# Experts' up product: from full-precision matmuls to three single-pass products of split tiles, with the rows turned one block sooner

## The reference, cut to what matters

```python
E, K, D, I = 16, 2, 512, 384
# x: [1250, 512]; each node goes to its two best of 16 experts, and all to a shared one
h = rows @ expert_w1[e] + expert_b1[e]          # up product: [n, 512] @ [512, 768]
g = clip(h[..., ::2], -gate_clamp, gate_clamp)
u = clip(h[..., 1::2], -up_clamp, up_clamp)
t = g * sigmoid(g * alpha) * gate_scale * (u + up_shift)
y = t @ expert_w2[e] + expert_b2[e]             # down product: [n, 384] @ [384, 512]
out[node] += weight * y
```

## Time and profile before

| | |
|---|---|
| median of 3 runs | 908.85 us |
| the profiled execution | 910.05 us, span 908.3 us |
| mean granted clock of PE | 0.926 |
| PE busy | 811.4 us, 89% |
| DVE busy | 485.9 us, 53% |
| ACT busy | 250.2 us, 28% |
| POOL busy | 126.6 us, 14% |
| experts' up product, L1224 | 448 matmul records, mean 492 ns, 155.9 us |
| experts' down product, L1272 | 168 records, mean 605 ns, 78.6 us |
| chain that ended last | PE 70%, DVE 17%, DMA 6%; L1224 14%, L1272 7% |

### The profile page before, as it was taken

How to read it: one execution, slowest core, us unless ns; L and a number is a source line. 1 busy time by engine, 2 the same in 40 slices (tenths; PEclk the granted TensorE clock), 3 DMA queues, 4 the chain that set the end, 5 groups by cost and what they waited for, 6 DMA issues and landing times.

```text
span 908.3 us, 12470 instructions
## 1 busy us (share of the span) xinstructions
PE 811.4 (89%) x3696; PEld 583.8 (64%) x3697; DVE 485.9 (53%) x949; ACT 250.2 (28%) x502; POOL 126.6 (14%) x186
## 2 busy tenths in 40 slices
PE   4679699999999986948999958989999999999993
PEld 2555588888888863626888846887655555555551
DVE  6899481441341387899024685896343443434341
ACT  2455241331341103515221313421021222212121
POOL 2000000000000120000000500212123333333321
PEclk9985699999999995979999968979999999999997
DMA  2600000000000010000101102004698859663542
GB/s 112 205 1 2 1 1 1 0 1 1 1 1 1 29 40 9 1 1 1 47 1 53 58 1 92 22 1 176 218 355 248 297 136 367 167 180 57 135 92 32
DMA packets 32156, 71.34 MB, mean 79 GB/s; under 512 B 4254, under 2 KB 4504, under 8 KB 32110
## 3 DMA queue, kind: packets, MB, share of 16 engines
q1 hardware_dynamic: 25838, 56.04, 17.1%
q0 software_dynamic: 6272, 14.68, 8.1%
HBM read 96.53 MB, written 12.72 MB: 120 GB/s over the span
## 4 chain that ended last, share of the span: by engine, by line
PE 70%; DVE 17%; DMA 6%; issue 3%; ACT 2%; SPq 1%; ACTq 0%; DVEq 0%; POOL 0%; POOLq 0%
PE PS L994 20%; PE PS L1224 14%; PE PS L1024 9%; PE PS L1272 7%; PE PS L1117 5%; PE PS L1063 3%; DMA WB<-in_w 3%; PE PS L925 3%; DMA X<-in_x 3%; PE PS L1257 2%; DVE XN L1343 1%; PE PS L1208 1%; DVE ET L1396 1%; DVE ET L1391 1%; ACT CTR L693 1%
## 5 line engine op out<-in xcount | busy, mean ns | idle before, releaser
L994 PE MATMUL PS<-CTR,YH 125*128 125x500 f32 (+1 forms) x480 | 164.1, 357 | 2.3 <-DVE YL L1526 2.3
L994 PE MATMUL PS<-CTR,YL 125*128 125x500 f32 (+1 forms) x480 | 163.6, 356 | 0.0
L1224 PE MATMUL PS<-WB,YF 128*128 x448 | 155.9, 492 | 0.1
L1224 PEld LDWEIGHTS PS<-WB,YF 128*128 128x128 f32 x448 | 80.9, 190 | 65.7 <-issue 20.7
L994 PEld LDWEIGHTS PS<-CTR,YH 125*128 125x128 f32 x480 | 91.5, 191 | 15.5 <-DVE YL L1526 2.6
L994 PEld LDWEIGHTS PS<-CTR,YL 125*128 125x128 f32 x480 | 91.5, 191 | 13.1
L925 PE MATMUL PS<-ET 125*128 125x130 f16 x494 | 66.4, 302 | 21.1 <-DVE ET L1401 17.2
L1272 PE MATMUL PS<-WB,YF 128*128 x168 | 78.6, 605 | 1.6 <-DMA WB<-in_w 0.9
L925 PEld LDWEIGHTS PS<-ET 125*128 125x128 f16 x494 | 43.2, 128 | 45.0 <-DVE ET L1401 22.2
L1553 DVE TENSOR_TENSOR ZL<-PS,ZH 128x500 fp32r<-128x500 f32 (+1 forms) x36 | 21.1, 592 | 90.1 <-ACT ZH L745 90.1
L648 POOL DMA_INDIRECT out<-YF,dest_i x28 | 44.6, 1591 | 73.5 <-ACT YF L891 48.4
(11 more groups left out here) (363 smaller groups left out, 1369.0 us busy)
## 6 DMA issues: line engine op xcount, KB each, us to landing
WB<-in_w SPq DMA_DIRECT2D x28, 1536.0 KB
WB<-in_w SPq DMA_DIRECT2D x28, 768.0 KB
WB<-in_b SPq DMA_DIRECT2D x28, 384.0 KB
X<-in_x SPq DMA_DIRECT2D x1, 2500.0 KB
xn_dram<-XN SPq DMA_DIRECT2D x1, 2500.0 KB
out<-X SPq DMA_DIRECT2D x10, 250.0 KB
WNEXT<-in_W SPq DMA_DIRECT2D x2, 1024.0 KB, 10.1
SR<-in_sw SPq DMA_DIRECT2D x1, 1536.0 KB, 7.8
```

Source lines behind the costliest of these rows:

```text
L994: mm = nc.tensor.matmul(dest, lhs, rhs, start=(t == 0 and h == 0), stop=(t == NT - 1 and h == 1))
L1224: mm = nc.tensor.matmul(PS[:, 2 * k + h, 0:INTER], xgt[:, k, f, :], WB[:, bass.ds(off + (f * H2 + h * INTER), INTER)], start=(f == 0), sto ...
```

## The change

- **Split weights.** Each block's w1, half by half, is cast on ACT to `W1H[k]` (`split_hi`) and the difference is made on DVE in `W1L[k]` (`split_lo`), both of 128 x 4 x 768. Every block is split, also one whose expert is that of the block before. `W1H[0]` and `W1L[0]` lie over scratch tiles, `W1H[1]` over X's tiles 0 to 5, and `W1L[1]` over X's tiles 6 to 9 and the start of the next region.
- **Split rows.** ACT casts the turned rows from bank 4 (`rows_hi`), DVE subtracts (`rows_lo`, in the place of `rows_copy`).
- **Products.** Per half, 12 single-pass matmuls of 384 columns instead of four float32 ones; the table read of the address goes from PE to ACT and DVE, once per half.
- **Order.** The rows of block b are turned before the up product of block b-1 instead of after it; `AHEAD` is 4. The first two pairs are written out, the loop starts at 3, and the last two blocks follow the loop. Every loop still runs to 17.
- **Stores of X.** The first six (`HEAD`) count on `out_head`, the others on `out_stored`. ACT waits for the first before it splits block 1, DVE for the others before its part.
- Small tables (`CWT`, `ohr`, `prodb`, `home`) have other places; new semaphores `xgt_hi`, `w1_hi`, `w1_lo`, `out_head`.

The diff, without the semaphores' and small tables' lines:

```diff
@@ -84,7 +84,8 @@
 KC = 81
 DOWN = (7, 3)
 ASSIGN = TOPK * NT
-AHEAD = 3
+AHEAD = 4
+HEAD = 6
 
...
@@ -345,6 +346,12 @@
         cw = invc[:, 0:NT * KC].rearrange("p (t e) -> p t e", t=NT)
         b2r = tmp[:, 0, :]
         SB1, SGL, SGH, SUL, SUH, SAB, SUB = 0, 2, 3, 4, 5, 6, 7
+
+        W1B = FT * H2 * 4
+        W1H = [at("W1H0", R_XN + ROWB - W1B, [128, FT, H2], F32R), at("W1H1", R_X, [128, FT, H2], F32R)]
+        W1L = [at("W1L0", R_YL + ROWB - W1B, [128, FT, H2], F32R), at("W1L1", R_X + W1B, [128, FT, H2], F32R)]
+        XGH = at("XGH", R_YH + 4096, [128, 2, FT, 128], F32R)
+        XGL = at("XGL", R_YL + 4096, [128, 2, FT, 128], F32R)
 
         rat = [2 * INTER]
...
@@ -504,7 +516,7 @@
                 load_weights(b // 2, b % 2, b)
             for t in range(NT):
                 sp.wait_ge(z_added, t + 1)
-                sp.dma_start(out[t * NP:(t + 1) * NP, :], X[0:NP, t, :]).then_inc(out_stored, 16)
+                sp.dma_start(out[t * NP:(t + 1) * NP, :], X[0:NP, t, :]).then_inc(out_head if t < HEAD else out_stored, 16)
             for b in range(FREE, 4):
                 load_weights(b // 2, b % 2, b)
             with sp.Fori(2, NB // 2) as i:
...
-                pool.wait_ge(out_stored, 16 * NT)
+                pool.wait_ge(out_head, 16 * HEAD)
+                pool.wait_ge(out_stored, 16 * (NT - HEAD))
                 pool.wait_ge(yo_ready, turn)
                 pool.wait_ge(dest_ready, turn)
                 pool.indirect_dma_start(out[:, :], bass.IndirectOffsetOnAxis(dest_i[:, k:k + 1], 0), yo[:, k, :], None,
@@ -652,17 +666,20 @@
                 gather(0, b % 2, b)
             pool.wait_ge(zeroed, 16)
             last = last_pair(pool)
-            gather(0, 1, AHEAD)
-            scatter(0, 0)
-            with pool.Fori(2, NB // 2) as i:
+
+            def pair(i):
+                gather(i, 0, i * 2)
+                scatter(0, i * 2 - AHEAD)
+                gather(i, 1, i * 2 + 1)
+                scatter(1, i * 2 + 1 - AHEAD)
+
+            pair(AHEAD // 2)
+            with pool.Fori(AHEAD // 2 + 1, NB // 2) as i:
                 with pool.If(i < last + 1):
-                    gather(i, 0, i * 2)
-                    scatter(1, i * 2 - AHEAD)
-                    gather(i, 1, i * 2 + 1)
-                    scatter(0, i * 2 + 1 - AHEAD)
-            ending = pool.value_load(eb_i[0:1, 3, 1:2], min_val=SURE - AHEAD, max_val=NB - AHEAD)
+                    pair(i)
+            end = ending(pool)
             for j in range(AHEAD):
-                scatter((j + 1) % 2, ending + j)
+                scatter(j % 2, end + j)
             pool.wait_ge(scattered, pool.to_reg(last * 32 + 32))
 
...
+
+            def rows_hi(k, b):
+                act.wait_ge(xt_ps, b + 1)
+                nc.scalar.copy(XGH[:, k, :, :], PS[:, 4, :].rearrange("p (f n) -> p f n", f=FT)).then_inc(xgt_hi, 1)
+
+            def split_hi(i, k, b, h):
+                off = act.value_load(eb_i[0:1, 1, bass.ds(b, 1)], min_val=0, max_val=(NWB - 1) * WBUF)
+                cols = slice(h * INTER, (h + 1) * INTER)
+                act.wait_ge(w1_in[k], i * 32 + 32)
+                if not (isinstance(b, int) and b < 2):
+                    act.wait_ge(hb_ready, b - 1)
+                raw = WB[:, bass.ds(off, FT * H2)].rearrange("p (f n) -> p f n", f=FT)
+                nc.scalar.copy(W1H[k][:, :, cols], raw[:, :, cols]).then_inc(w1_hi, 1)
+
+            def pair(i):
+                rows_hi(0, i * 2)
+                sigmoid(0, i * 2 - 2)
+                split_hi(i, 0, i * 2, 0)
+                if not (isinstance(i, int) and i < 2):
+                    result(1, i * 2 - 3)
+                split_hi(i, 0, i * 2, 1)
+                turn_t(0, i * 2 - 2)
+                rows_hi(1, i * 2 + 1)
+                sigmoid(1, i * 2 - 1)
+                split_hi(i, 1, i * 2 + 1, 0)
+                result(0, i * 2 - 2)
+                split_hi(i, 1, i * 2 + 1, 1)
+                turn_t(1, i * 2 - 1)
+
+            split_hi(0, 0, 0, 0)
+            split_hi(0, 0, 0, 1)
+            act.wait_ge(out_head, 16 * HEAD)
+            split_hi(0, 1, 1, 0)
+            split_hi(0, 1, 1, 1)
+            rows_hi(0, 0)
+            rows_hi(1, 1)
+            pair(1)
+            pair(2)
+            with act.Fori(3, NB // 2) as i:
                 with act.If(i < last + 1):
-                    turn_t(1, i * 2 - 1)
-                    sigmoid(0, i * 2)
-                    with act.If(i < 2):
-                        result(0, 1, 1, first=True)
-                    with act.If(i > 1):
-                        result(i - 1, 1, i * 2 - 1)
-                    turn_t(0, i * 2)
-                    sigmoid(1, i * 2 + 1)
-                    result(i, 0, i * 2)
-            turn_t(1, last * 2 + 1)
-            result(last, 1, last * 2 + 1)
+                    pair(i)
+            end = ending(act)
+            sigmoid(0, end + 2)
+            result(1, end + 1)
+            turn_t(0, end + 2)
+            sigmoid(1, end + 3)
+            result(0, end + 2)
+            turn_t(1, end + 3)
+            result(1, end + 3)
 
...
@@ -1204,6 +1255,8 @@
 
             def turn_rows(i, k, b):
                 pe.wait_ge(gathered[k], i * 16 + 16)
+                if not (isinstance(b, int) and b < 1):
+                    pe.wait_ge(xgt_ready, b)
                 for f in range(FT):
                     mm = nc.tensor.transpose(PS[:, 4, f * 128:(f + 1) * 128], xg[:, k, f * 128:(f + 1) * 128], ident[:, :])
                 mm.then_inc(xt_ps, 1)
@@ -1212,18 +1265,18 @@
                 if not (isinstance(p, int) and p < 2):
                     pe.wait_ge(clip_done, p - 1)
 
-            def up(i, k, b, between):
-                off = pe.value_load(eb_i[0:1, 1, bass.ds(b, 1)], min_val=0, max_val=(NWB - 1) * WBUF)
-                pe.wait_ge(w1_in[k], i * 32 + 32)
+            def up(k, b, between):
                 pe.wait_ge(xgt_ready, b + 1)
                 up_bank_free(b)
                 for h in range(2):
                     if h and between:
                         between()
+                    cols = slice(h * INTER, (h + 1) * INTER)
+                    pe.wait_ge(w1_lo, b * 2 + (h + 1))
                     for f in range(FT):
-                        mm = nc.tensor.matmul(PS[:, 2 * k + h, 0:INTER], xgt[:, k, f, :],
-                                              WB[:, bass.ds(off + (f * H2 + h * INTER), INTER)],
-                                              start=(f == 0), stop=(f == FT - 1))
+                        for j, (x, wt) in enumerate(((XGH, W1H), (XGL, W1H), (XGH, W1L))):
+                            mm = nc.tensor.matmul(PS[:, 2 * k + h, 0:INTER], x[:, k, f, :], wt[k][:, f, cols],
+                                                  start=(f == 0 and j == 0), stop=(f == FT - 1 and j == 2))
                 mm.then_inc(hb_ready, 1)
 
             def turn_act(k, p):
...
+            up(0, 0, None)
             pe.wait_ge(z_added, EARLY)
-            up(0, 1, 1, lambda: turn_act(0, 0))
-            pe.wait_ge(xgt_ready, 2)
-            turn_rows(1, 0, 2)
-            down(0, 0, 0)
-            with pe.Fori(1, NB // 2) as i:
+
+            def pair(i):
+                turn_rows(i, 0, i * 2)
+                if not (isinstance(i, int) and i < 2):
+                    down(i - 2, 1, i * 2 - 3)
+                up(1, i * 2 - 1, lambda: turn_act(0, i * 2 - 2))
+                turn_rows(i, 1, i * 2 + 1)
+                down(i - 1, 0, i * 2 - 2)
+                up(0, i * 2, lambda: turn_act(1, i * 2 - 1))
+
+            pair(1)
+            pair(2)
+            with pe.Fori(3, NB // 2) as i:
                 with pe.If(i < last + 1):
-                    up(i, 0, i * 2, lambda: turn_act(1, i * 2 - 1))
-                    turn_rows(i, 1, i * 2 + 1)
-                    with pe.If(i < 2):
-                        down(0, 1, 1)
-                    with pe.If(i > 1):
-                        down(i - 1, 1, i * 2 - 1)
-                    up(i, 1, i * 2 + 1, lambda: turn_act(0, i * 2))
-                    with pe.If(i < last):
-                        turn_rows(i + 1, 0, i * 2 + 2)
-                    down(i, 0, i * 2)
-
-            turn_act(1, last * 2 + 1)
-            down(last, 1, last * 2 + 1)
+                    pair(i)
+            end = ending(pe)
+            down(last - 1, 1, end + 1)
+            up(1, end + 3, lambda: turn_act(0, end + 2))
+            down(last, 0, end + 2)
+            turn_act(1, end + 3)
+            down(last, 1, end + 3)
 
 
...
@@ -1833,9 +1887,18 @@
             ins.then_inc(sel_ready, 1)
 
 
-            def rows_copy(k, b):
-                dve.wait_ge(xt_ps, b + 1)
-                v.tensor_copy(xgt[:, k, :, :], PS[:, 4, :].rearrange("p (f n) -> p f n", f=FT)).then_inc(xgt_ready, 1)
+            def rows_lo(k, b):
+                dve.wait_ge(xgt_hi, b + 1)
+                v.tensor_tensor(XGL[:, k, :, :], PS[:, 4, :].rearrange("p (f n) -> p f n", f=FT), f32(XGH[:, k, :, :]),
```

(38 more changed lines are left out.)

39 lines of the change are left out of this document (23 added, 16 removed).

## The result

The changed kernel takes 925.78 us (median of 4 runs, 925.48 to 928.62), the kernel before 909.34 (4 runs, 907.89 to 910.51). The ratio is 1.0189, with a 95% interval of 1.0163 to 1.0214: 16.4 us slower. The forecast was 7.9 slower, at 916.8, with a range of 900 to 928.

The account below looks back on a forecast made before the run. PE bounds the experts' stage before; after, a loop through ACT and DVE at 8.36 us a block. The 18.6 us lost at the start, 25 such steps and the end make +7.9 on 908.85: 916.8, range 900 to 928.

Parts of the forecast that it names:

- the sum: Whole kernel: start loss, 25 steps of 8.36 us and the end give +7.9 us on the median of 908.85, 916.8.
- PE's up halves: PE's up product in the experts' stage: each half in 2.15 us, with single-pass matmuls of 384 columns at 0.180 us.
- The loop: Experts' stage: clip, sigmoid, roundings on ACT and subtractions on DVE set steps of 8.15 and 8.57 us, 8.36 a block.
- The start: First blocks: ACT and DVE wait for X's stores before splitting block 1; 18.6 us lost, its clip at 677.2.
- The end: Last two blocks: empty loop turns and a table read put block 26's clip at 888.4, block 27's 6.6 us later.
- rival 2: POOL's gathers come late to PE's row transposes, 0.7 to 1.5 us on half the blocks: about 927 us, chance 0.18.
- The lead of 6.1 us: Experts' stage: time from a gather's issue on POOL to PE's transposes wanting it, with PE's slack of 0.7 on top.
- The price of a late gather: Experts' stage: if POOL's copies wait for subtractions, half of the 26 blocks are 0.7 to 1.5 us late, +9 or more.
- The prediction's own sign of being wrong: Experts' stage: the forecast is wrong if PE waits at its row transposes for gathers; no size given.
- The row about ports: DVE's product at L1782 took 1.29 us beside a POOL subtraction, against 0.62 on 384 elements, so it waited for POOL.

Follow-up runs that it names:

- the first experiment: The changed kernel with POOL issuing the gather of block b+1 ahead of the scatter of block b-4 instead of behind it: 915.4 us, ratio 1.0077.

## Why the prediction was right or wrong

**The sign was right, and so were the two mechanisms of the sum:** PE's product got faster, and a loop through ACT and DVE took PE's place as the bound. PE's up halves take 2.1 us (12 matmuls, forecast 2.15). Of the 28 clips 7 still wait for PE: those of blocks 1, 4, 5, 9, 14, 18 and 27, among them the three at the end of the long steps.

**The loop.** Forecast steps 8.15 and 8.57, mean 8.36; measured 8.06 and 8.33, mean 8.20. The rounding starts 2.54 after the clip (forecast 2.77) and the two subtractions run back to back. The kernel with the subtraction cut to 8 columns shows that the register work on DVE is what ends last, as the earlier trace rows had let one expect. Moving the reads gives 0.4 on every other step (8.07 to 7.64), and turning DVE's loop 0.7 on the others (8.33 to about 7.6). The mean was over by 0.16, 4 us over 25 steps.

**The start.** Forecast: block 0's up product 661.2, block 1's clip 677.2, against 658.57 before. Measured 659.73 and 675.8. DVE's subtraction behind the last store's landing started at 664.20 (forecast 665.2 + 0.9).

**The end.** The step to block 26's clip over the empty turns took 11.54 (forecast 8.36 + 2.2), the last 6.86 (forecast 6.6).

**The step that failed is rival 2's place outside the sum.** Its mechanism was right: the gather behind the scatter on POOL, the copies that wait for subtractions. But the sum counted late gathers at nothing, and they cost about 10 us of the 16.4. The lead of 6.1 us was worked out for a scatter that goes 1.4 after the result; where the scatter before is still in flight it goes when that has landed, and the earlier trace rows had no row for a scatter's landing. With 8.67 us of landing and a copy of 1.60 the gather of the longest step left 4.4 us before PE wanted it (775.07 against 779.44), and it flew 8.1. The price of a late gather was too small too: I took the lateness alone, 0.7 to 1.5 us on half the blocks. In the trace few blocks are late, but a wait of 3.8 us makes a step 7 us longer, because the clock falls with it. That rival 2's 927 is near the measured time is luck: it spread small delays over half of the blocks, where three steps have nearly all of it. The prediction's own sign of being wrong, PE waiting at its row transposes for gathers, is what the trace shows.

From the trace: block 1's clip to block 26's is 224.0 us, forecast 211.2; 24 steps of 8.20 and the end's 11.5 make 208.3, and of the 15.7 left the three long steps have 13.9. In medians the first experiment gives 10.4; the profiled run of the changed kernel was itself 2.8 over its median. With the late gathers away, 915.4 stands beside a forecast of 916.8. Part of that agreement is two errors that cancel: in that run the 24 steps are 2.8 us shorter than forecast, and the end is 1.4 longer.

**The row about ports** was read too strongly. At the same width of 500 columns two of DVE's products at L1782 with no subtraction of POOL's beside them took 0.73 us, so the one of 1.29 was 0.56 longer; the 0.62 it was held against is of another line with 384 columns. The direction holds.

**What stays open.** Why the step at block 5 is 11.6 even with the short subtraction and 9.9 with the early copy was not tried apart; that the chain alone would do it is an assumption. How the rest of the 10.4 divides between GpSimd's longer instructions (7.3 when taken away) and the chain's other links is not shown, since both act on the same waits.

## What to carry to other kernels

When work is moved onto DVE and ACT, follow the small instructions of the engine that feeds them too: a chain through the landing of a DMA (scatter, landing, index copy, scatter, gather) has no slack shown by any busy share, and it takes the place of the bound where only two result buffers stand ahead of it, as here. Issue gathers ahead of the scatter that may wait, and fill index tiles before the wait and not behind it. Count register reads as work of the engine where they stand between two waits, and move them under a wait.
